# Gated attention and mixture of experts: the residual sum as two fused VectorE operations, the state products as 32-row blocks

## The chip, the cores and the metric

The kernel runs on one core of one Trainium2 chip. The metric is the device time of one execution in microseconds (us); lower is better. The core has the engines TensorE (PE in the profile, with its weight loads as PEld), VectorE (DVE), ScalarE (ACT), GpSimd (POOL) and SyncE (SP), which run side by side and wait for one another by semaphores, and 16 DMA engines.

## What is computed

Inputs are `x` (8 sequences of 512 tokens, 256 wide) and a context of the same shape. The first half, cut to what matters:

```python
q = layernorm(x); k = v = context
ig, fg = gates of [q, k, v], one per head         # 8 heads of 32
cs = cumsum(log_sigmoid(fg)); log_D = causal(cs_s - cs_t + ig_t)
C = (q_h @ k_h.T / sqrt(32)) * exp(log_D - rowmax)
h = (C / (max(|sum C|, exp(-rowmax)) + eps)) @ v_h
x = x + tanh(g0) * layernorm(h) * ln_scale
```

The second half is a mixture of 9 experts (256 to 704 to 256, the two best of 9 per token) on `layernorm(x)`, added with weight `tanh(g1)`.

## The kernel before, in words

**Stages.** A first stage (0 to 57 us) normalises the queries and makes the gate products. A gate stage (57 to about 70 us) makes the cumulative sums and the factors. The **slot loop** (about 77 to 302 us) does the attention for 32 tiles of 128 tokens, tile t = 4b + c being quarter c of sequence b, and beside it splits the experts' weights into two bf16 parts and writes them back to memory. A short routing stage (302 to 350 us) picks experts and builds gather tables. The expert stage (350 to 788 us) gathers tokens, multiplies and scatters, with TensorE nearly always busy.

**The slot loop's order.** The order on each engine is written out by hand in `slot_pe`, `slot_act`, `slot_dve`, `slot_pool` and `slot_sync` (lines 739 to 816). Every engine runs strictly through its own list, slot by slot; there is no planner. A tile is spread over several slots: in slot t, VectorE finishes the attention of tile t (`b_h_dve`), takes statistics of `h` of tile t and of the residual sum of tile t-2 (`c_sth_dve`, `c_stx_dve`), updates the running state of tile t+1 (`b_st_dve`), and multiplies and splits the scores of tile t+2 (`b_c_dve`, `b_cl_dve`: Cm at line 588, Cl at line 596). Line 625, the first operation of `b_h_dve`, is a good mark for where a slot begins on VectorE; it waits for TensorE's products of tile t (lines 522 to 537), which may start only when the `h` of tile t-1 has been taken out of PSUM (`b_ho`).

**ScalarE** in slot t normalises `h` of tile t-1 into `x2` (`c_hn_act`, line 682), normalises tile t-3 into `y`, takes the exponentials of tile t+2, copies, makes the two factors `rs` (`c_rs_act`), casts the scores to bf16 (Ch, line 550) and then casts one 128x1224 piece of the weights (line 468).

**GpSimd** in slot t makes `kw` of tile t+2 (line 569), `qE` of tile t+1 (577), the low part of the values (561), the residual sum of tile t-1 in two operations (`c_pool`: times `lsg` at 717, plus `xc` at 720), and then three operations on the piece of weights that ScalarE just cast (`w_pool`, line 483).

**The state.** For each tile but the last of a sequence, TensorE multiplies `kw` (128 tokens by 4 heads x 32) with the values (128 tokens by 4 heads x 33) for two groups of four heads (lines 498 to 500). Each 128x132 result holds 16 blocks of head by head, of which only the four on the diagonal are wanted. VectorE scales the result and zeroes the rest with the mask `blkm`: for c = 0 straight into the state `St` (line 607), for c = 1 and 2 into `Ut` (line 609), from which two operations update the state (line 615: `St_new = St_old * dec + Ut`). c = 3 has no update. The state is the moving operand of line 522.

**The start.** Constants are made on GpSimd (`consts_pool`) and VectorE (`consts_dve`). ScalarE and TensorE wait for all of them (`s_const` at NCONST) before anything else. In the gate stage, `g_dvef` on VectorE and `g_pool` on GpSimd work at the same time.

The functions that the change touches, and those that call them:

Of the kernel before, what the change touches and what calls it, by code (L numbers as in the profile page):

```python
# [60 lines left out]
def build(nc, x, kv, wgate, fib, lnrow, gsc, wroute, rbias, wts, out):  # L61
    with ExitStack() as ctx:
# [18 lines left out]
        rowj = sb("rowj", [P, P]); rowjb = sb("rowjb", [P, P], BF16); pairj = sb("pairj", [P, HALF]); pcol = sb("pcol", [P, 1]); blk = sb("blk", [P, HG * DV])  # L81
# [4 lines left out]
        selt = sb("selt", [12, HG]); blkm = sb("blkm", [P, HG * DV]); blkt = sb("blkt", [P, HG * DV])  # L86
# [27 lines left out]
        Ut = attn("Ut", [P, 2, HG * DV])  # L114
# [48 lines left out]
        b_kw = sem("b_kw"); b_ut = sem("b_ut"); b_st = sem("b_st")  # L163
# [47 lines left out]
        NCONST = 16  # L211

        def consts_dve(dve):
            nc.vector.memset(eps_c[:, :], LN_EPS).then_inc(s_const, 1)
# [9 lines left out]
            nc.vector.tensor_scalar(blkt[:, :], blk[:, :], float(DH), pcol[:, 0:1], ALU.add, ALU.is_gt).then_inc(s_const, 1)  # L224
            nc.vector.tensor_scalar(blkm[:, :], blk[:, :], pcol[:, 0:1], None, ALU.is_le).then_inc(s_const, 1)
            dve.wait_ge(s_const, 11)
            nc.vector.tensor_tensor(blkm[:, :], blkm[:, :], blkt[:, :], ALU.mult).then_inc(s_const, 1)
# [449 lines left out]
        def c_hn_act(act, t):  # L677
            c = t % NC
            ge(act, c_nb, t + 1)
            ge(act, c_y, t - 3)  # L680
            ge(act, c_x2o[c], 16 * (t // NC))
            nc.scalar.activation(x2[:, c, :], h[:, c, :], ACT.Identity, bias=nb[:, c, 0:1], scale=rs[:, c, 0:1]).then_inc(c_xn, 1)
# [9 lines left out]
        def c_rs_act(act, t):  # L692
# [19 lines left out]

        def c_pool(pool, t):
            G = nc.gpsimd
            b, c = t // NC, t % NC
            ge(pool, c_xn, t + 1)
            G.tensor_tensor(x2[:, c, :], x2[:, c, :], lsg[:, :], ALU.mult).then_inc(c_xa, 1)  # L717
            ge(pool, c_xa, t + 1)
            ge(pool, c_x[b % 2], 16 * (b // 2) + 16)
            G.tensor_tensor(x2[:, c, :], x2[:, c, :], xc[b % 2][:, c, :], ALU.add).then_inc(c_x2, 1)  # L720
# [70 lines left out]
        def slot_pool(pool, t):  # L791
# [646 lines left out]
```

## Time and profile before

| | us |
|---|---|
| median of 3 runs | 788.55 (786.97 to 788.75) |
| the profiled execution, its own time | 790.31 |
| span of the profiled execution | 788.5 |
| VectorE busy | 527.2 (67%) |
| GpSimd busy | 404.8 (51%) |
| TensorE busy | 678.9 (86%) |
| ScalarE busy | 386.1 (49%) |

The profile is of one execution. Busy time is the time in which an engine had an instruction in work; a busy TensorE is not TensorE at its peak, since its instructions overlap. Fp32 products have two records each for the weight load and for the product. The shares above are means over stages with different limits, so a change in the slot loop is read from the slot loop. The granted clock of TensorE is 1.00 for 2.4 GHz and 0.50 for 1.2 GHz.

### The profile page before, as it was taken

What the parts mean: (1) busy time and instruction counts of PE and PEld (TensorE: products, weight loads), DVE (VectorE), ACT (ScalarE), POOL (GpSimd) and SP (SyncE); (2) the same over time, 40 slices, a digit from 0 to 9 for tenths busy, and PEclk for the clock granted to TensorE, in tenths of its full rate; (3) what the DMA queues carried; (4) which work ended last, traced back from release to release, by engine and by line L of the source; (5) the groups of instructions that cost most, each with busy time, mean ns of one, the idle gap of its engine ahead of it and who ended that gap; (6) DMA issues with size and microseconds to landing.
All of it is one profiled execution on the core that took longest, in us unless ns stands there. A gap on an engine that the chain in (4) does not pass through costs nothing.

```text
span 788.5 us, 17816 instructions
## 1 busy us (share of the span) xinstructions
PE 678.9 (86%) x6018; PEld 545.5 (69%) x6018; DVE 527.2 (67%) x1389; ACT 386.1 (49%) x973; POOL 404.8 (51%) x402
## 2 busy tenths in 40 slices
PE   1983889998899874068999999999999999999993
PEld 1541556665566663047998989988989899889893
DVE  8716899899998877964555565555555555655551
ACT  3533677777777763154344444343444443434441
POOL 5024499897989991021244453453444535444423
PEclk9995655557655655569999999999999999999997
DMA  9813789986998861173597897897988977969752
GB/s 283 270 37 122 198 267 263 297 280 208 298 300 254 269 209 54 29 307 108 166 289 238 265 281 253 232 315 213 281 259 245 291 253 234 315 200 305 231 147 49
DMA packets 85817, 179.70 MB, mean 228 GB/s; under 512 B 14881, under 2 KB 48546, under 8 KB 85730
## 3 DMA queue, kind: packets, MB, share of 16 engines
q1 hardware_dynamic: 63202, 140.10, 56.2%
q0 software_dynamic: 13824, 18.43, 10.8%
q10 hardware_dynamic: 8704, 20.06, 6.5%
q8 instruction: 48, 0.79, 0.4%
q14 instruction: 39, 0.32, 0.1%
HBM read 140.93 MB, written 38.67 MB: 228 GB/s over the span
## 4 chain that ended last, share of the span: by engine, by line
PE 57%; POOL 20%; issue 9%; DVE 9%; ACT 2%; DMA 2%; SPq 1%; POOLq 0%; DVEq 0%; ACTq 0%
PE bank L1096 49%; POOL whl L483 8%; POOL x L717 3%; POOL x L720 3%; POOL vp L561 3%; POOL qE L577 2%; PE bank L304 2%; PE bank L1090 2%; PE bank L307 2%; POOL kw L569 2%; DVE R L991 1%; PE bank L317 1%; DMA EB<-e_d 1%; DVE Qe L988 1%; PE bank L734 1%
## 5 line engine op out<-in xcount | busy, mean ns | idle before, releaser
L1096 PE MATMUL bank<-xh,w 128*128 128x256 bf16 (+1 forms) x1760 | 268.2, 263 | 9.7 <-DVE xl L1152 5.7
L1078 POOL DMA_INDIRECT out<-res,TS x72 | 115.4, 1603 | 214.9 <-DVE res L1213 130.9
L1096 PE MATMUL bank<-xl,w 128*128 128x256 bf16 (+1 forms) x880 | 222.5, 263 | 0.0
L1169 ACT ACTIVATE sg<-bank 128x256 f32<-128x256 f32 (+1 forms) x240 | 86.8, 362 | 230.3 <-PE bank L1096 226.6
L1096 PEld LDWEIGHTS bank<-xh,w 128*128 128x128 bf16 x1760 | 165.5, 98 | 28.5 <-issue 11.9
L1199 DVE TENSOR_TENSOR hf<-sg,bank 128x256 f32<-128x256 f32 (+1 forms) x200 | 78.9, 394 | 122.5 <-ACT sg L1169 117.4
L1096 PE MATMUL bank<-w,hh 128*128 128x256 bf16 x864 | 140.0, 273 | 0.0
L483 POOL TENSOR_TENSOR whl<-wst,whl 128x408 bf16<-128x408 f32 x96 | 94.0, 1006 | 61.2 <-ACT whl L468 61.1
L1069 POOL DMA_INDIRECT xg<-y_d,TG x72 | 72.7, 1010 | 79.0 <-DVE TS L1026 48.4
L1096 PE MATMUL bank<-w,hlo 128*128 128x256 bf16 x360 | 98.1, 273 | 0.0
L1163 ACT CAST hh<-hf 128x256 bf16<-128x256 f32 (+1 forms) x240 | 90.4, 377 | 12.9 <-DVE hf L1201 11.6
L1096 PEld LDWEIGHTS bank<-xl,w 128*128 128x128 bf16 x880 | 86.4, 98 | 8.3
L1096 PEld LDWEIGHTS bank<-w,hh 128*128 128x128 bf16 x864 | 84.5, 98 | 9.3
L1185 DVE TENSOR_TENSOR hlo<-hf,hh 128x256 bf16<-128x256 f32 (+1 forms) x200 | 78.3, 392 | 0.0
L596 DVE TENSOR_TENSOR Cl<-Cm,Ch 128x512 bf16<-128x512 f32 x64 | 60.3, 979 | 7.3 <-ACT Ch L550 5.0
L1213 DVE TENSOR_SCALAR res<-bank,cws 128x256 f32<-128x256 f32 x72 | 31.8, 479 | 43.2 <-PE bank L1096 43.2
L550 ACT CAST Ch<-Cm 128x512 bf16<-128x512 f32 x64 | 37.0, 617 | 39.6 <-DVE Cm L588 39.6
L510 PE MATMUL bank<-maskb,identb 128*128 128x512 bf16 x64 | 36.3, 567 | 14.4 <-ACT Dm L544 10.0
L588 DVE SCALAR_TENSOR_TENSOR Cm<-bank,Dm 128x512 f32<-128x512 f32 x64 | 41.1, 680 | 7.6 <-ACT Dm L544 7.6
L734 PEld LDWEIGHTS bank<-wr,yT 128*128 128x128 f32 x128 | 27.8, 303 | 20.8 <-ACT yT L706 11.4
L468 ACT CAST whl<-wst 128x1224 bf16<-128x1224 f32 x32 | 38.6, 1209 | 4.2 <-DMA w_d<-whl 4.2
L734 PE MATMUL bank<-wr,yT 128*128 128x9 f32 x128 | 30.7, 351 | 9.0 <-ACT yT L706 8.0
(222 smaller groups left out, 1107.4 us busy)
## 6 DMA issues: line engine op xcount, KB each, us to landing
w<-w_d SPq DMA_DIRECT2D x40, 1408.0 KB
w<-w_d SPq DMA_DIRECT2D x40, 768.0 KB
wst<-in_wts SPq DMA_DIRECT2D x32, 612.0 KB, 4.7
w_d<-whl ACTq DMA_DIRECT2D x32, 612.0 KB, 6.7
vb<-in_kv SPq DMA_DIRECT2D x8, 528.0 KB, 5.4
xa<-in_x SPq DMA_DIRECT2D x8, 512.0 KB, 8.5
kT<-in_kv SPq DMA_DIRECT2D x8, 512.0 KB, 8.9
xc<-in_x SPq DMA_DIRECT2D x8, 512.0 KB, 7.7
```

Of the source, the lines that this page charges most:

```text
L468: nc.scalar.copy(whl[w][:, 0, :], wst[w][:, :]).then_inc(w_hi, 1)
L483: ins = nc.gpsimd.tensor_tensor(whl[w][:, 1, cols], wst[w][:, cols], whl[w][:, 0, cols], ALU.subtract)
L588: nc.vector.scalar_tensor_tensor(by4(Cm[t % 2][g][:, :]), bank[:, 4:8, g * P:(g + 1) * P], SCALE, by4(Dm[t % 2][g][:, :]), ALU.mult, ALU.m ...
L596: nc.vector.tensor_tensor(Cl[k][:, :], Cm[t % 2][g][:, :], Ch[k][:, :], ALU.subtract).then_inc(b_Cl, 1)
L734: mm = nc.tensor.matmul(bank[:, 3, LG0 + c * NE:LG0 + (c + 1) * NE], yT[t % 2][:, k, :], wr[:, k, :], start=(k == 0), stop=(k == KD - 1))
L1069: nc.gpsimd.indirect_dma_start(xg[w][:, j, :], None, y_d, bass.IndirectOffsetOnAxis(ap=TG[:, c0:c0 + 1], axis=0)).then_inc(f_xg[w], 16)
L1078: nc.gpsimd.indirect_dma_start(out, bass.IndirectOffsetOnAxis(ap=TS[:, c0:c0 + 1], axis=0), res[w][:, j, :], None, bounds_check=TOK - 1, o ...
L1096: mm = nc.tensor.matmul(dst, l, r, start=(n == 0), stop=(n == len(pairs) - 1))
L1163: nc.scalar.copy(hh[w][0:K, m, 0:N], hf[m % 3][0:K, 0:N]).then_inc(f_hh, 1)
L1169: nc.scalar.activation(sg[m % 2][0:K, 0:N], bank[0:K, 2 + (NM * w + m) % 4, 0:N], ACT.Silu).then_inc(f_sg, 1)
L1185: V.tensor_tensor(hl_[w][:, m, 0:N], hf[m % 3][:, 0:N], hh[w][:, m, 0:N], ALU.subtract).then_inc(f_hl, 1)
L1199: V.tensor_tensor(hf[m % 3][:, 0:N], sg[m % 2][:, 0:N], bank[:, bk, SLOT:SLOT + N], ALU.mult).then_inc(f_hf, 1)
```

## The change

Two things change in the slot loop.

1. `c_hn_act` on ScalarE and `c_pool` on GpSimd go. In their place, `c_x2_dve` on VectorE makes `x2 = (h - mean) * lsg` and `x2 = x2 * rs + xc`, two `scalar_tensor_tensor` operations of 128x256, the second waiting for the first. It stands in `slot_dve` right behind `b_h_dve`, for tile t-1.
2. The state product is made by eight products of 32 output rows and 33 columns, one per head, straight into the diagonal blocks. The rest of the PSUM region is zeroed once, in the gate stage. The mask, `Ut` and line 609 go, the update reads PSUM directly, and the factor SCALE moves into the copy that makes `col` (line 348). With the mask go one `iota` on GpSimd and three operations on VectorE among the constants, and NCONST is 13.

```diff
+            V.memset(bank[:, 4:6, UO:UO + HG * DV], 0.0).then_inc(b_uz, 1)
...
-                    nc.scalar.copy(dst, src).then_inc(g_cols, 1)
+                    nc.scalar.activation(dst, src, ACT.Copy, scale=SCALE).then_inc(g_cols, 1)
...
                 for g in range(2):
-                    mm = nc.tensor.matmul(bank[:, 4 + g, UO:UO + HG * DV], kw[u % 2][:, g * P:(g + 1) * P],
-                                          vv(u)[:, g * HG * DV:(g + 1) * HG * DV], start=True, stop=True)
+                    for j in range(HG):
+                        hd = g * HG + j
+                        mm = nc.tensor.matmul(bank[DH * j:DH * (j + 1), 4 + g, UO + DV * j:UO + DV * (j + 1)],
+                                              kw[u % 2][:, DH * hd:DH * (hd + 1)], vv(u)[:, DV * hd:DV * (hd + 1)],
+                                              start=True, stop=True)
...
                 ub = bank[:, 4:6, UO:UO + HG * DV]
-                mask = blkm[:, :].unsqueeze(1).to_broadcast([P, 2, HG * DV])
+                ge(dve, b_h, t)
                 if c == 0:
-                    ge(dve, b_h, t)
-                    V.scalar_tensor_tensor(St[0][:, :, :], ub, SCALE, mask, ALU.mult, ALU.mult).then_inc(b_st, 1)
+                    V.tensor_copy(St[0][:, :, :], ub).then_inc(b_st, 1)
                 else:
-                    V.scalar_tensor_tensor(Ut[:, :, :], ub, SCALE, mask, ALU.mult, ALU.mult).then_inc(b_ut, 1)
                     if t == 1:
                         ge(dve, s_dec, 16 * HG)
-                    ge(dve, b_ut, b * 2 + c)
-                    ge(dve, b_h, t)
                     for g in range(2):
                         ins = V.scalar_tensor_tensor(St[c % 2][:, g, :], St[1 - c % 2][:, g, :], dec[:, b, g, c:c + 1],
-                                                     Ut[:, g, :], ALU.mult, ALU.add)
+                                                     ub[:, g, :], ALU.mult, ALU.add)
...
+        def c_x2_dve(dve, t):
+            V = nc.vector
+            b, c = t // NC, t % NC
+            ge(dve, c_rs, t + 1)
+            ge(dve, c_mv2, t + 1)
+            ge(dve, c_y, t - 3)
+            ge(dve, c_x2o[c], 16 * b)
+            V.scalar_tensor_tensor(x2[:, c, :], h[:, c, :], mv[:, c, 0, 0:1], lsg[:, :], ALU.subtract, ALU.mult).then_inc(c_xn, 1)
+            ge(dve, c_xn, t + 1)
+            ge(dve, c_x[b % 2], 16 * (b // 2) + 16)
+            V.scalar_tensor_tensor(x2[:, c, :], x2[:, c, :], rs[:, c, 0:1], xc[b % 2][:, c, :], ALU.mult, ALU.add).then_inc(c_x2, 1)
...
         def slot_dve(dve, t):
             if 0 <= t < NT:
                 b_h_dve(dve, t)
+            if 0 <= t - 1 < NT:
+                c_x2_dve(dve, t - 1)
             if 0 <= t < NT:
                 c_sth_dve(dve, t)
```

The calls of `c_hn_act` in `slot_act` and of `c_pool` in `slot_pool` are removed with the functions.

## Rows read from the trace of the kernel before

**Rows 1.** Busy us (x count) of PE, PEld, DVE, ACT, POOL; PEclk, DMA, GB/s

```profile
95.80:291.20 195.40, 179.89 (x1571) 122.52 (x1567) 177.41 (x422) 148.47 (x314) 176.55 (x210) 0.56 0.87 268
110.00:153.00 43.00, 41.92 (x340) 28.09 (x336) 39.33 (x95) 32.33 (x68) 38.88 (x47) 0.50 0.96 295
...
258.00:265.00 7.00, 4.62 (x57) 2.92 (x56) 6.79 (x17) 5.18 (x11) 5.28 (x8) 0.97 1.03 317
```

**Rows 2.** Chain of waits of the slot loop, shares by line

```profile
by line: POOL whl L483 29.0%; issue 25.2%; POOL x L717 11.3%; POOL x L720 10.5%; POOL vp L561 9.5%; POOL qE L577 8.0%; POOL kw L569 6.5%; POOLq L182 0.4%
```

**Rows 3.** Line 607, one in four slots: min/median/max, first and last start

```profile
L607 DVE SCALAR_TENSOR_TENSOR St<-bank,blkm x8: 415/433/433, 81.4 to 270.7; 128x264 f32<-128x264 f32 x8
```

**Rows 4.** VectorE in order of time: start, us, line; from 199.71 one whole slot

```profile
199.71 0.15 DVE L625 SCALAR_TENSOR_TENSOR n<-bank,col 128x8 f32<-128x8 f32 x1
...
200.34 0.42 DVE L632 TENSOR_TENSOR h<-bank,n 128x256 f32<-128x256 f32 x1
...
201.88 0.40 DVE L609 SCALAR_TENSOR_TENSOR Ut<-bank,blkm 128x264 f32<-128x264 f32 x1
202.31 1.09 DVE L615 SCALAR_TENSOR_TENSOR St<-St,dec,Ut 128x132 f32<-128x132 f32 x2
203.33 1.27 DVE L588 SCALAR_TENSOR_TENSOR Cm<-bank,Dm 128x512 f32<-128x512 f32 x2
...
204.82 1.79 DVE L596 TENSOR_TENSOR Cl<-Cm,Ch 128x512 bf16<-128x512 f32 x2
206.53 0.15 DVE L625 SCALAR_TENSOR_TENSOR n<-bank,col 128x8 f32<-128x8 f32 x1
...
217.57 2.20 DVE L596 TENSOR_TENSOR Cl<-Cm,Ch 128x512 bf16<-128x512 f32 x2 [0.15 <-ACT Ch L550]
```

**Rows 5.** VectorE again, where GpSimd was idle

```profile
87.14 0.62 DVE L615 SCALAR_TENSOR_TENSOR St<-St,dec,Ut 128x132 f32<-128x132 f32 x2
...
288.17 1.29 DVE L596 TENSOR_TENSOR Cl<-Cm,Ch 128x512 bf16<-128x512 f32 x2
```

**Rows 6.** GpSimd in order of time

```profile
204.73 0.73 POOL L720 TENSOR_TENSOR x<-x,xc 128x256 f32<-128x256 f32 x1
206.45 2.81 POOL L483 TENSOR_TENSOR whl<-wst,whl 128x408 bf16<-128x408 f32 x3 [0.99 <-ACT whl L468]
```

**Rows 7.** ScalarE in order of time

```profile
288.51 1.21 ACT L468 CAST whl<-wst 128x1224 bf16<-128x1224 f32 x1
```

**Rows 8.** VectorE by line and shape, whole span: busy us, mean ns

```profile
L1185 DVE TENSOR_TENSOR hlo<-hf,hh 128x256 bf16<-128x256 f32 x160 | 66.8, 418 | 0.0
L596 DVE TENSOR_TENSOR Cl<-Cm,Ch 128x512 bf16<-128x512 f32 x64 | 60.3, 979 | 7.3 <-ACT Ch L550 5.0
...
L1213 DVE TENSOR_SCALAR res<-bank,cws 128x256 f32<-128x256 f32 x72 | 31.8, 479 | 43.2 <-PE bank L1096 43.2
...
L615 DVE SCALAR_TENSOR_TENSOR St<-St,dec,Ut 128x132 f32<-128x132 f32 x32 | 18.6, 622 | 0.6
```

**Rows 9.** TensorE in order of time at the half clock

```profile
210.12 1.02 PE L734 MATMUL bank<-wr,yT 128*128 128x9 f32 x4
...
213.15 1.24 PE L493 MATMUL bank<-qT,kT 32*128 32x128 f32 x16
214.32 1.25 PE L499 MATMUL bank<-vb,kw 128*128 128x132 f32 x4
```

**Rows 10.** GpSimd, then VectorE, in the constants at the start

```profile
6.93 3.65 POOL L208 MEMSET mx<- 24x4096 bf16 x1
...
7.05 3.61 DVE L225 TENSOR_SCALAR blkm<-blk,pcol 128x132 f32<-128x132 f32 x1
10.70 0.30 DVE L227 TENSOR_TENSOR blkm<-blkm,blkt 128x132 f32<-128x132 f32 x1
```

**Rows 11.** VectorE in the gate stage

```profile
63.79 0.17 DVE L384 MEMSET g<- 64x128 f32 x1
63.89 1.36 DVE L385 TENSOR_TENSOR g<-gm 64x384 f32<-64x384 f32 x1
```

More of the change, by code:

```diff
@@ L78, in build @@
         bank = ctx.enter_context(nc.psum_tensor("bank", [P, 8, 512], F32))
-        rowj = sb("rowj", [P, P]); rowjb = sb("rowjb", [P, P], BF16); pairj = sb("pairj", [P, HALF]); pcol = sb("pcol", [P, 1]); blk = sb("blk", [P, HG * DV])
+        rowj = sb("rowj", [P, P]); rowjb = sb("rowjb", [P, P], BF16); pairj = sb("pairj", [P, HALF]); pcol = sb("pcol", [P, 1]);
         tokp1 = sb("tokp1", [P, NT])
@@ L85, in build @@
         maskb = sb("maskb", [P, P], BF16); sel12 = sb("sel12", [12, HG])
-        selt = sb("selt", [12, HG]); blkm = sb("blkm", [P, HG * DV]); blkt = sb("blkt", [P, HG * DV])
+        selt = sb("selt", [12, HG]);
         eps_c = sb("eps_c", [P, 1]); neps_c = sb("neps_c", [P, 1]); revj = sb("revj", [P, NE]); one_c = sb("one_c", [P, 1])
@@ L113, in build @@
         kw = [attn(f"kw{w}", [P, D]) for w in range(2)]; St = [attn(f"St{w}", [P, 2, HG * DV]) for w in range(2)]
-        Ut = attn("Ut", [P, 2, HG * DV])
         n1 = attn("n1", [P, NH]); n2 = attn("n2", [P, NH]); n3 = attn("n3", [P, NH])
@@ L162, in build @@
         b_dl = sem("b_dl"); b_s = sem("b_s"); b_D = sem("b_D"); b_C = sem("b_C")
-        b_kw = sem("b_kw"); b_ut = sem("b_ut"); b_st = sem("b_st")
+        b_kw = sem("b_kw"); b_uz = sem("b_uz"); b_st = sem("b_st")
         b_h = sem("b_h"); b_n = sem("b_n"); b_ho = sem("b_ho")
@@ L168, in build @@
         c_x = [sem(f"c_x{w}") for w in range(2)]; c_st2 = sem("c_st2"); c_mv2 = sem("c_mv2"); c_st3 = sem("c_st3"); c_mv3 = sem("c_mv3")
-        c_nb = sem("c_nb"); c_lv = sem("c_lv"); c_rs = sem("c_rs"); c_xa = sem("c_xa"); c_xn = sem("c_xn"); c_x2 = sem("c_x2"); c_y = sem("c_y"); c_yT = sem("c_yT"); c_yc = sem("c_yc")
+        c_nb = sem("c_nb"); c_lv = sem("c_lv"); c_rs = sem("c_rs"); c_xn = sem("c_xn"); c_x2 = sem("c_x2"); c_y = sem("c_y"); c_yT = sem("c_yT"); c_yc = sem("c_yc")
         c_lp = sem("c_lp"); c_lg = sem("c_lg"); c_x2o = [sem(f"c_x2o{c}") for c in range(NC)]; c_yo = [sem(f"c_yo{c}") for c in range(NC)]
@@ L199, in consts_pool @@
                            allow_small_or_imprecise_dtypes=True).then_inc(s_iota, 1)
-            nc.gpsimd.iota(blk[:, :].rearrange("p (h e) -> p h e", e=DV), [[DH, HG], [0, DV]], base=0,
-                           channel_multiplier=0, allow_small_or_imprecise_dtypes=True).then_inc(s_iota, 1)
             nc.gpsimd.iota(tokp1[:, :], [[P, NT]], base=1, channel_multiplier=1,
@@ L209, in consts_pool @@
                 nc.gpsimd.memset(asb[w][:, :, :], 1.0).then_inc(s_mz, 1)
-        NCONST = 16
+        NCONST = 13
         def consts_dve(dve):
@@ L217, in consts_dve @@
             nc.vector.memset(onesb[:, :], 1.0).then_inc(s_const, 1)
-            dve.wait_ge(s_iota, 5)
+            dve.wait_ge(s_iota, 4)
             nc.vector.tensor_copy(rowjb[:, :], rowj[:, :]).then_inc(s_const, 1)
@@ L223, in consts_dve @@
             nc.vector.tensor_scalar(maskb[:, :], rowj[:, :], pcol[:, 0:1], NEG, ALU.is_lt, ALU.mult).then_inc(s_const, 1)
[L224 to L227, printed above, removed]
+            dve.wait_ge(s_const, 9)
             nc.vector.tensor_tensor(selt[:, :], identf[0:12, 0:4], identf[0:12, 4:8], ALU.add).then_inc(s_const, 1)
-            dve.wait_ge(s_const, 13)
+            dve.wait_ge(s_const, 10)
             nc.vector.tensor_tensor(sel12[:, :], selt[:, :], identf[0:12, 8:12], ALU.add).then_inc(s_const, 1)
@@ L358, in g_pe_all @@
             mm.then_inc(g_col, 1)
+            pe.wait_ge(b_uz, 1)
             b_s_pe(pe, 0)
@@ L675, in c_nb_dve @@
             nc.vector.scalar_tensor_tensor(nb[:, r, lo:hi], mv[:, r, lo:hi, 0], -1.0, rs[:, r, lo:hi], ALU.mult, ALU.mult).then_inc(c_nb, 1)
[L677 to L682, printed above, removed]
+        def c_x2_dve(dve, t):
[9 more added lines that the diff above has]
+            V.scalar_tensor_tensor(x2[:, c, :], x2[:, c, :], rs[:, c, 0:1], xc[b % 2][:, c, :], ALU.mult, ALU.add).then_inc(c_x2, 1)
         def c_y_act(act, t):
@@ L696, in c_rs_act @@
             ge(act, c_mv3, t - 1)
-            ge(act, c_xn, t - 3)
+            ge(act, c_x2, t - 3)
             ge(act, c_y, t - 5)
@@ L711, in c_lg_act @@
                            bank[:, 3, LG0:LG0 + NC * NE]).then_inc(c_lg, 1)
[L713 to L720, printed above, removed]
         def c_T_pe(pe, t):
@@ L751, in slot_act @@
         def slot_act(act, t):
-            if 0 <= t - 1 < NT:
-                c_hn_act(act, t - 1)
             if 0 <= t - 3 < NT:
@@ L797, in slot_pool @@
                 b_v_pool(pool, t + 1)
-            if 0 <= t - 1 < NT:
-                c_pool(pool, t - 1)
             if t in PIECE:
```

## The prediction

> **What bounds the kernel now.** The change touches the slot loop and a little of the start, so I first asked for the busy time of that loop alone. Over 195.4 us VectorE is busy 177.4, GpSimd 176.6 and TensorE 179.9 [rows 1]: three engines at about 91%, ScalarE at 76%. No single engine is clearly the bound, and the page's shares for the whole span (67% and 51%) hide this. TensorE runs the loop mostly at a granted clock of about half (mean 0.56); where it was 0.50 throughout, TensorE was busy 41.92 of 43.00 us, where it was 0.97 only 4.62 of 7.00 [rows 1]. The chain of waits lies on GpSimd from end to end, 29.0% on line 483 and 21.8% on the two operations that the change removes [rows 2]. That invites the reading "unload GpSimd and the loop gets faster". Whether it holds depends on what the other engines have left, so I took the pitch of the loop: line 607 runs once in four slots, eight times from 81.4 to 270.7, which is 189.3 / 28 = 6.76 us a slot [rows 3].
>
> Next, VectorE in order of time [rows 4]. In the slot from 199.71 to 206.53 it has no idle time of note: 2.17 us from line 625 to line 609, 1.45 for Ut and the two state operations, 1.49 from Cm to Cl, 1.71 for the two Cl. So VectorE has no room for more work; only the length of its own operations can give.
>
> They can give, for this reason: an operation of VectorE with two SBUF operands waits while GpSimd's is in work. The pair of Cl took 1.29 us and the pair of St 0.62 where GpSimd was idle [rows 5], but 1.79 and 1.09 in the slot above [rows 4]. The Cl pair of 204.82 shows how: GpSimd's line 720 ran from 204.73 to 205.46 and then GpSimd was idle until 206.45 [rows 6], and the pair was longer by just the rest of that one operation. Over all slots Cl has a mean of 979 ns against some 0.65 alone, St 622 against 0.31 [rows 5, 8]. In the constants the same shows at its largest: line 225 stood 3.61 us behind GpSimd's memset of 3.65 [rows 10].
>
> **The change, part by part**, per slot on VectorE.
>
> 1. Two new operations. A 128x256 operation with two SBUF operands alone took 418 ns (line 1185); a pointer scalar adds about 60, by line 1213 (479) [rows 8]. So 2 x 0.48, and 0.05 for the hand-over between them: +1.0.
> 2. What they wait for GpSimd. The pair starts 1.05 us behind line 625 (200.34 + 0.42 against 199.71) [rows 4]. When does GpSimd's burst of line 483 start? It follows ScalarE's weight cast, which ended at 289.72 where the Cl pair ended at 289.46 [rows 5, 7], so about 0.3 us behind the start of the slot, now that nothing else keeps GpSimd. The burst is 2.8 us long [rows 6]. So the pair falls into it in every slot: the first operation waits for the rest of one 0.94 us operation (some 0.2 to 0.4), and the second, which may start only when the first is done, for most of the next (0.5). Bounds: 0 if they miss the burst, and 1.2 (the Cl pair of 217.57 took 2.20, 0.9 more than alone [rows 4, 5], beside operations of 0.73; beside those of 0.94 that is 0.9 x 0.94 / 0.73). I take +0.8, as the phase puts the pair inside.
> 3. Ut goes: 0.43 in half of the slots [rows 4]: -0.2.
> 4. St reads PSUM instead of Ut and no longer has two SBUF operands. As the Cm of line 588, which also mixes PSUM and SBUF and keeps 1.27 for its pair [rows 4], it should keep its length alone. From 2 x 0.62 to 0.62 in half of the slots [rows 5, 8]: -0.3. For c = 0 a copy replaces an operation of 433 ns [rows 3]: 0.
> 5. Cl. GpSimd's list shrinks by two operations of 0.73 alone [rows 6], from about 6.1 us (176.6 in the 28.9 slots of [rows 1]) to 4.5, plus some 0.8 that it waits for the pair. It starts at 0.3 and ends near 5.6, while the Cl pair starts 1.3 us before the end of the slot. So Cl is free: from 2 x 0.98 to 1.29: -0.65 [rows 5, 8].
> 6. Idle time of VectorE that the longer list absorbs: -0.1.
>
> Sum: 1.0 + 0.8 - 0.2 - 0.3 - 0.65 - 0.1 = +0.55, say +0.5 a slot, over some 30 slots **+15 us**. The other moves: `c_hn_act` leaves ScalarE, which had 24% idle, so 0; its place in the list is ahead of work that waits for VectorE anyway. No DMA is added or moved; the store of `x2` waits for the same sum, which now comes at most a slot later or earlier, with two slots to spare. New waits (`c_rs`, `c_mv2`, the stores) are for things of the slot before: 0. What queues behind the pair is the statistics, then `rs` on ScalarE, then Cm; `rs` is wanted only behind Cm: 0.
>
> **TensorE.** At the half clock it is busy 41.92 of 43.00 us [rows 1], 6.6 a slot, so it is as full as VectorE. Eight products of a quarter width replace two. The nearest row is line 493: eight products on a quarter of the array each, 16 records in 1.24 us [rows 9], about what line 499 takes now. I take 0. Below: 0.3, a quarter of line 499's 1.25, if four run side by side; that gain would be hidden behind VectorE. Above: 4.1, if each costs like a product of line 734, of which two, with few columns, take 1.02 [rows 9]. With a slot of 7.3 TensorE has 0.7 left, over three products in four slots 0.9 for each: it stays hidden up to some 2.1 us.
>
> **The start.** VectorE's line 227 (0.30) goes, with an iota of GpSimd ahead of its memsets. Line 225 goes too, but line 229 behind it has two SBUF operands and would stand behind the same memset [rows 10]: -0.3 for line 227; the iota comes on top, unpriced. The new memset in the gate stage (264 columns; the one ahead of it, of 128, took 0.17, so about 0.3) goes ahead of line 385, which took 1.36 us, mostly a wait for GpSimd [rows 11]; that wait covers it: 0, and +0.3 without this cover.
>
> **Sum.** 15 - 0.3 = +14.7. The profiled execution took 790.31 (span 788.5), 1.8 above the median; from it 805.0, and against the median of 788.55, 803.
>
> **A rule weighed.** Alone, an operation of two SBUF operands took 0.645 us with 512 columns (the Cl pair halved) and 0.418 with 256, 0.89 ns a column, which gives 0.31 for 132; the St pair, of the new operations' form, took 0.31 each [rows 5, 8]. At half the rate it would be 0.42. The Trainium skill, Vector Engine (DVE) Microarchitecture Reference, "Points that are easy to get wrong", says that this form of instruction with two SBUF sources that aren't bf16 runs at half the throughput. By it each new operation would be longer by 256 columns' time, and the sum about 14 us higher; by the rows it is not. This is the third rival below.
>
> **The rivals.**
> - *The pair misses the burst* (faster). Place: 1.05 us into a VectorE slot. If the weight cast comes late on ScalarE, or the slot's start is early, the pair runs while GpSimd is idle, at 1.0. Then the slot is 6.76 + 1.0 - 0.2 - 0.3 - 0.65 = 6.6, or -5 us in all with the start: 783. It decides at 0.3 us of wait for the pair. For it: GpSimd's share of busy time falls to about 70%. Against: the phase of rows 5 and 7. Chance 0.17.
> - *Nothing to measure*: the wait for the pair is 0.2 to 0.4: 786 to 791. Chance 0.13.
> - *Half throughput* in the new operations: 256 columns more at 0.89 ns, 0.23 each, 0.46 a slot, +14 on top: 817. Against: the St pair. Chance 0.06.
> - *TensorE becomes the bound*: the eight products take more than 2.1 us at the half clock. Halfway to the upper bound, at 2.6, a slot takes 6.6 + 0.75 x (2.6 - 1.2) = 7.65: +0.9 over 30 slots, 815; at 4.1 it is 8.8 a slot, 850. Against: rows 9, line 493. Chance 0.05.
> - My forecast: 0.59.
>
> That the change does nothing is no rival: the operations leave GpSimd by name.
>
> **The numbers.** Forecast 803. The range of 785 to 815 holds my forecast with its bounds (a pair's wait of 0.4 to 1.2), the case of no difference and the edge of the first rival; it leaves out the rest of that and most of the last two, 0.2. A measurement here can tell 0.3% from no change, 2.4 us. Faster 0.17, no difference 0.13, slower 0.59 + 0.06 + 0.05 = 0.70.
>
> **What would show it.** GpSimd's busy time in the loop down by some 50 us. Line 596 at a mean near 0.7 us, line 615 near 0.33. The two new operations at 0.48 alone but 0.7 to 1.0 in the mean, more in the second. The pitch of four slots near 29 us, with VectorE waiting for nobody. Wrong would be: the pair at 1.0 to 1.2 (first rival), VectorE idle before line 625 behind TensorE (the last), or Cl still near 1.0, which would add up to 0.65 a slot.

## The result, and the profile after

The changed kernel takes **791.82 us** (median of 20 runs, 788.08 to 801.65), the kernel before 788.46 in runs beside it (20 runs, 785.82 to 790.64). The 801.65 is a slow execution, at a granted clock of 0.794 where the other 19 have 0.814 to 0.834, and the ratio leaves it out. The ratio is 1.0041, with a 95% interval of 1.0028 to 1.0055: slower by 0.41%, just more than the 0.3% that a measurement here can tell. The forecast was 803 with a range of 785 to 815. The direction and the range held; the size did not: +3.4 us where the sum said +14.7.

The profiled execution of the changed kernel took 794.40 us (span 792.3), 2.6 above the median; that of the kernel before lies 1.8 above its own, so the two traces can be compared.

The busy time of the slot loop, in the columns of [rows 1], over the same stretch:

```profile
95.80:291.20 195.40, 164.41 (x1792) 107.58 (x1788) 183.56 (x458) 133.45 (x284) 129.93 (x152) 0.59 0.86 267
```

GpSimd went from 176.6 us to 129.9, -46.7 where some -50 was forecast, and VectorE from 177.4 to 183.6 of 195.4. TensorE fell from 179.9 to 164.4. VectorE is now the one full engine. The chain of waits from 95.8 to 245 says so too; in [rows 2] nearly every share was GpSimd's, and in the list below none is. (Over the whole stretch of [rows 2], 95.8 to 292, the chain has 8.7% on GpSimd's line 479 and 13.2% on Cl.)

```profile
by line: issue 25.0%; DVE Cl L595 17.3%; DVE x L679 9.6%; ACT Ch L549 8.0%; DVE st L648 5.6%; DVE Cm L587 5.1%; ACTq L470 3.4%; DVE st L657 3.3%; DVE n L624 3.0%; DVE n L622 2.5%; DVEq L181 2.1%; DVE x L682 1.9%; ACT lv L699 1.8%; DVE mv L6
```

(The list goes on behind its last entry.) The pitch by the line that runs once in four slots [rows 3] is (273.4 - 80.8) / 28 = 6.88 us against 6.76:

```profile
L605 DVE COPY St<-bank x8: 411/413/433, 80.8 to 273.4; 128x264 f32<-128x264 f32 x8
```

One slot of VectorE in order of time, to be read against [rows 4], and beside it GpSimd, to be read against [rows 6]:

```profile
200.05 0.42 DVE L627 TENSOR_TENSOR h<-bank,n 128x256 f32<-128x256 f32 x1
200.39 0.69 DVE L679 SCALAR_TENSOR_TENSOR x<-h,mv,lsg 128x256 f32<-128x256 f32 x1
201.11 1.06 DVE L682 SCALAR_TENSOR_TENSOR x<-x,rs,xc 128x256 f32<-128x256 f32 x1
202.10 0.41 DVE L648 BATCH_NORM_STATS2 st<-h 128x6 f32<-128x256 f32 x1
...
203.17 0.59 DVE L610 SCALAR_TENSOR_TENSOR St<-St,dec,bank 128x132 f32<-128x132 f32 x2
203.68 1.28 DVE L587 SCALAR_TENSOR_TENSOR Cm<-bank,Dm 128x512 f32<-128x512 f32 x2
...
205.18 1.29 DVE L595 TENSOR_TENSOR Cl<-Cm,Ch 128x512 bf16<-128x512 f32 x2
206.39 0.16 DVE L620 SCALAR_TENSOR_TENSOR n<-bank,col 128x8 f32<-128x8 f32 x1
```

```profile
199.84 3.15 POOL L479 TENSOR_TENSOR whl<-wst,whl 128x408 bf16<-128x408 f32 x3 [1.91 <-ACT whl L464]
202.95 0.72 POOL L576 TENSOR_TENSOR qE<-qT,EB 128x256 f32<-128x256 f32 x1
203.64 0.68 POOL L560 TENSOR_TENSOR vp<-vb,vp 128x264 bf16<-128x264 f32 x1
```

The slot starts at 199.42 (the first n of line 620), the burst at 199.84, 0.42 us in (forecast: 0.3). The pair of new operations (lines 679 and 682) lies wholly inside it. It takes 202.10 - 200.39 = 1.71 us from its start to the start of what follows. Where GpSimd was idle, at the end of the loop, the same pair took 0.91:

```profile
297.40 0.42 DVE L627 TENSOR_TENSOR h<-bank,n 128x256 f32<-128x256 f32 x1
297.75 0.47 DVE L679 SCALAR_TENSOR_TENSOR x<-h,mv,lsg 128x256 f32<-128x256 f32 x1
298.26 0.48 DVE L682 SCALAR_TENSOR_TENSOR x<-x,rs,xc 128x256 f32<-128x256 f32 x1
298.66 0.42 DVE L648 BATCH_NORM_STATS2 st<-h 128x6 f32<-128x256 f32 x1
```

GpSimd pays for the meeting too: three operations of line 479 take 3.15 us here against 2.81 in [rows 6]. The Cl pair, by contrast, runs after GpSimd's list has ended (204.32) and takes its 1.29. The means over all slots agree (VectorE, 96 to 292; columns as in [rows 8], where the means are of the whole span). First the kernel before, then the changed one:

```profile
L596 DVE TENSOR_TENSOR Cl<-Cm,Ch 128x512 bf16<-128x512 f32 x58 | 56.0, 1005 | 7.0 <-ACT Ch L550 5.0
...
L615 DVE SCALAR_TENSOR_TENSOR St<-St,dec,Ut 128x132 f32<-128x132 f32 x28 | 16.7, 635 | 0.5
...
L625 DVE SCALAR_TENSOR_TENSOR n<-bank,col 128x8 f32<-128x8 f32 x29 | 4.7, 160 | 3.8 <-PE bank L536 3.2
```

```profile
L595 DVE TENSOR_TENSOR Cl<-Cm,Ch 128x512 bf16<-128x512 f32 x56 | 36.6, 695 | 5.3 <-ACT Ch L549 2.9 <-PE bank L535 0.2
...
L682 DVE SCALAR_TENSOR_TENSOR x<-x,rs,xc 128x256 f32<-128x256 f32 x28 | 29.1, 1041 | 1.0
L679 DVE SCALAR_TENSOR_TENSOR x<-h,mv,lsg 128x256 f32<-128x256 f32 x29 | 19.6, 676 | 0.0
...
L610 DVE SCALAR_TENSOR_TENSOR St<-St,dec,bank 128x132 f32<-128x132 f32 x28 | 8.3, 339 | 0.0
...
L620 DVE SCALAR_TENSOR_TENSOR n<-bank,col 128x8 f32<-128x8 f32 x28 | 4.5, 160 | 0.3 <-PE bank L535 0.3
```

The last column is idle time of VectorE before the operation: its wait for TensorE at the start of a slot fell from 3.8 us to 0.3, and its wait ahead of Cl from 7.0 to 5.3.

**Where the time went.** A record's duration is not the time that it holds up the engine, because records overlap (run 6 below has 0.39 us of record in 0.31 of time). So the account is in times from start to start, as means over all slots from 96 to 292 in the timeline of VectorE:

| us a slot | before | after | difference |
|---|---|---|---|
| first n to h | 0.63 | 0.63 | 0 |
| h to the statistics of h (with the pair) | 0.46 | 2.02 | +1.56 |
| the statistics | 1.18 | 1.11 | -0.07 |
| state update (with Ut, before) to Cm | 0.87 | 0.35 | -0.52 |
| Cm to Cl | 1.70 | 1.61 | -0.08 |
| Cl to the next n | 2.02 | 1.24 | -0.78 |
| pitch | 6.86 | 6.96 | +0.10 |

The ends of the loop do the rest. The first n comes 0.37 us earlier (84.25 against 84.62); the last state copy, at 273.4, 2.7 later; the last n (296.77 against 295.35) only 1.4 later, as the last slots take less time than before; and what follows the loop on VectorE (302.93 against 300.61) 2.3 later. The first gather of the expert stage keeps these 2.3 (351.38 against 349.07). The spans differ by 3.8 (792.3 and 788.5), so 1.5 arises in the expert stage, which the change doesn't touch and which no run took apart; the spans of 19 executions of the changed kernel lie up to 6 us apart (786.2 to 792.3), so these 1.5 may be no effect of the change.

TensorE's side of the change, in order of time, against [rows 9]:

```profile
213.20 1.24 PE L489 MATMUL bank<-qT,kT 32*128 32x128 f32 x16
214.37 0.45 PE L497 MATMUL bank<-vb,kw 128*32 128x33 f32 x16
214.75 0.61 PE L509 MATMUL bank<-maskb,identb 128*128 128x512 bf16 x1
```

The eight products take 214.75 - 214.37 = 0.38 us, start to start; two of full width took 1.04 (the next operation began at 215.36 after 214.32), both at a granted clock of 0.50.

### The profile page after: what moved, and what is told of

The parts are those of the page before. It is cut to its first block, busy times and chain, and to the rows that moved or that the text cites. A ratio compares the mean times of both kernels' runs of the same rounds, so it can differ in the third digit from the quotient of the medians.

```text
span 792.3 us, 18373 instructions
## 1 busy us (share of the span) xinstructions
PE 665.5 (84%) x6306; PEld 531.9 (67%) x6306; DVE 538.3 (68%) x1435; ACT 371.6 (47%) x941; POOL 353.9 (45%) x337
## 4 chain that ended last, share of the span: by engine, by line
PE 54%; DVE 21%; issue 10%; ACT 4%; DMA 4%; POOL 4%; ACTq 1%; DVEq 0%; SPq 0%; POOLq 0%
PE bank L1085 44%; DVE Cl L595 4%; DMA out<-res,TS 4%; POOL whl L479 2%; DVE x L679 2%; PE bank L298 2%; PE bank L301 2%; ACT Ch L549 2%; PE bank L1079 1%; DVE Cm L587 1%; DVE st L648 1%; DVE R L980 1%; PE bank L311 1%; DVE xl L1141 1%; PE bank L725 1%
## 5 line engine op out<-in xcount | busy, mean ns | idle before, releaser
L479 POOL TENSOR_TENSOR whl<-wst,whl 128x408 bf16<-128x408 f32 x96 | 99.5, 1064 | 110.8 <-ACT whl L464 107.3
L595 DVE TENSOR_TENSOR Cl<-Cm,Ch 128x512 bf16<-128x512 f32 x64 | 42.4, 702 | 5.8 <-ACT Ch L549 2.9
L489 PE MATMUL bank<-qT,kT 32*128 32x128 f32 x512 | 39.2, 450 | 1.2 <-DVE Cm L587 1.2
```

The lines of the kernel that those rows point to most:

```text
L479: ins = nc.gpsimd.tensor_tensor(whl[w][:, 1, cols], wst[w][:, cols], whl[w][:, 0, cols], ALU.subtract)
L489: mm = nc.tensor.matmul(bank[:, 4 + j, g * P:(g + 1) * P], kT[rows, b, c, g * P:(g + 1) * P], qT[rows, b, c, g * P:(g + 1) * P], start=Tru ...
L595: nc.vector.tensor_tensor(Cl[k][:, :], Cm[t % 2][g][:, :], Ch[k][:, :], ALU.subtract).then_inc(b_Cl, 1)
```

## The experiments

The kernel before ran beside every group of runs, at a median of 788.7 to 788.9. The diffs are cut to the lines that matter; where a run leaves out or adds more than its diff shows, the text says so. The means from start to start come from VectorE's timeline as in the table above.

**1. The residual sum alone.** The kernel before, with only the residual sum moved to VectorE (`c_hn_act` goes as well); the state product with mask and Ut stays.

```
         def slot_dve(dve, t):
             if 0 <= t < NT:
                 b_h_dve(dve, t)
+            if 0 <= t - 1 < NT:
+                c_x2_dve(dve, t - 1)
...
-            if 0 <= t - 1 < NT:
-                c_pool(pool, t - 1)
```

> The kernel before with the residual sum on VectorE alone; state product, mask and Ut as before. Theory A (VectorE's list sets the pitch of the slot loop, and the new pair costs it 0.80 us alone plus 0.76 of waiting for GpSimd's burst): the pitch is that of the changed kernel, 6.96 us, plus Ut (0.43 in half of the slots) and the St pair's wait (0 to 0.3), so 7.2 to 7.4, and the time 797 to 804 us. Theory B (another engine, TensorE above all, holds the pitch near 6.9, and VectorE only fills it): 789 to 793, the same as the changed kernel.

Measured: 809.18 us, 1.0261 [1.0235 to 1.0288]; pitch 7.47. That is above the range of the theory, and far from its rival. The theory gave Ut 0.2 us a slot and the St pair's wait 0 to 0.3. VectorE's timeline has more:

```profile
202.96 0.67 DVE L684 SCALAR_TENSOR_TENSOR x<-h,mv,lsg 128x256 f32<-128x256 f32 x1
203.66 1.06 DVE L687 SCALAR_TENSOR_TENSOR x<-x,rs,xc 128x256 f32<-128x256 f32 x1
...
205.72 0.40 DVE L609 SCALAR_TENSOR_TENSOR Ut<-bank,blkm 128x264 f32<-128x264 f32 x1
206.16 1.49 DVE L615 SCALAR_TENSOR_TENSOR St<-St,dec,Ut 128x132 f32<-128x132 f32 x2
```

The state update, which reads two SBUF operands here, stands in its turn behind GpSimd: 1.49 us for what took 0.62 alone [rows 5]. From the first state operation to Cm it is 0.90 us a slot in the mean, against 0.35 in the changed kernel. From Cl to the next n it is 1.22, and VectorE waits for TensorE nowhere at the start of a slot (0.0 us), though TensorE still makes the two full products. The residual sum by itself costs 20.5 us, not 3.4. The changed kernel is nearly level only because its other half pays for it.

**2. The state blocks alone.** The changed kernel, with the residual sum put back to ScalarE and GpSimd.

```
-            V.scalar_tensor_tensor(x2[:, c, :], h[:, c, :], mv[:, c, 0, 0:1], lsg[:, :], ALU.subtract, ALU.mult).then_inc(c_xn, 1)
...
+            nc.scalar.activation(x2[:, c, :], h[:, c, :], ACT.Identity, bias=nb[:, c, 0:1], scale=rs[:, c, 0:1]).then_inc(c_xn, 1)
...
+            G.tensor_tensor(x2[:, c, :], x2[:, c, :], lsg[:, :], ALU.mult).then_inc(c_xa, 1)
```

> The kernel before with the state product in 32-row blocks alone; the residual sum stays on ScalarE and GpSimd. Theory A: VectorE is relieved of Ut (0.2 a slot) and of the St pair's wait (0.3), so the pitch goes from 6.86 to 6.4 to 6.6, time 777 to 783 us; GpSimd, busy 6.1 us a slot, is the next limit and may keep part of it. Theory B: TensorE is relieved too, by 0.66 us in three of four slots (eight products took 0.38 where two took 1.04), so 0.5 a slot, and the time also falls, but then TensorE shows idle time of less than 0.3 us a slot.

Measured: 778.69 us, 0.988 [0.9851 to 0.9909], as the theory said; again, later (label e12), 779.58, 0.9891 [0.9864 to 0.9917]:

> The same kernel as e2_state_only: 778 to 780 us, 1.2% under the kernel before.

The loop in the columns of [rows 1], then VectorE's Cl by line:

```profile
95.80:281.00 185.20, 168.63 (x1790) 111.93 (x1790) 167.72 (x405) 146.65 (x312) 181.30 (x210) 0.55 0.90 280
```

```profile
L595 DVE TENSOR_TENSOR Cl<-Cm,Ch 128x512 bf16<-128x512 f32 x56 | 60.8, 1124 | 10.8 <-ACT Ch L549 9.0
```

The pitch is 6.56 and GpSimd is busy 181.3 of 185.2 us (168.1 before): now it is the fullest engine. VectorE saved 0.51 between update and Cm, and 0.28 came back: 0.17 from Cm to Cl, where the wait for ScalarE's Ch has grown from 5.0 to 9.0 us, and 0.11 from Cl to n. Cl has a mean of 1124 ns, against 1013 in the kernel before over the same stretch (96 to 281); GpSimd was in work during 1.08 us of a Cl operation in the mean, during 0.77 before. The run relieves TensorE too, by 0.66 us in three slots of four, and how much of the 10 us is due to that, it doesn't show. So the two halves of the change don't add: -10 and +20.5 alone (+10.5), +3.4 together.

**3. The pair at another place.** The changed kernel, with the pair moved from behind h to ahead of Cl.

```
         def slot_dve(dve, t):
             if 0 <= t < NT:
                 b_h_dve(dve, t)
-            if 0 <= t - 1 < NT:
-                c_x2_dve(dve, t - 1)
...
                 c_nb_dve(dve, t)
+            if 0 <= t - 1 < NT:
+                c_x2_dve(dve, t - 1)
             if 0 <= t + 2 < NT:
```

> The changed kernel with the two operations of the residual sum moved from behind b_h_dve to ahead of the Cl pair in VectorE's list, where GpSimd was idle in the trace. Theory A: the pair takes 0.48 + 0.48 us instead of 0.68 + 1.04, Cl stays near 0.65 to 0.75 each, the pitch falls by 0.5 to 0.75 to 6.2 to 6.45, time 773 to 780 us. Theory B: the pair is as short, but VectorE shows the time as idle (ahead of line 620, behind TensorE), and the time stays at 786 to 792.

Measured: 781.49 us, 0.9912 [0.9887 to 0.9938], 10 us less than the changed kernel, with the same instructions; 1.5 above the range expected. VectorE's timeline shows a slot where the pair meets the end of GpSimd's list, and the next, where it doesn't; the second fence is GpSimd:

```profile
200.36 0.55 DVE L670 SCALAR_TENSOR_TENSOR nb<-mv,rs 128x2 f32<-128x2 f32 x1
200.84 0.98 DVE L679 SCALAR_TENSOR_TENSOR x<-h,mv,lsg 128x256 f32<-128x256 f32 x1
201.86 0.48 DVE L682 SCALAR_TENSOR_TENSOR x<-x,rs,xc 128x256 f32<-128x256 f32 x1
...
208.14 0.15 DVE L670 SCALAR_TENSOR_TENSOR nb<-mv,rs 128x2 f32<-128x2 f32 x1
208.21 0.48 DVE L679 SCALAR_TENSOR_TENSOR x<-h,mv,lsg 128x256 f32<-128x256 f32 x1
208.72 0.48 DVE L682 SCALAR_TENSOR_TENSOR x<-x,rs,xc 128x256 f32<-128x256 f32 x1
```

```profile
200.16 0.73 POOL L576 TENSOR_TENSOR qE<-qT,EB 128x256 f32<-128x256 f32 x1
200.85 0.69 POOL L560 TENSOR_TENSOR vp<-vb,vp 128x264 bf16<-128x264 f32 x1
...
206.57 0.68 POOL L560 TENSOR_TENSOR vp<-vb,vp 128x264 bf16<-128x264 f32 x1
```

At 208.21 GpSimd has been idle since 207.25 and both operations take 0.48. At 200.84 the first stands beside vp of line 560 and is 0.50 us longer. It is the same pair, and only GpSimd's work beside it differs. In this kernel VectorE is busy 177.4 of 185.2 us and its idle time, but for the hand-overs of some 0.03 us between its own operations, is 1.0 us in all: VectorE's list, with what is left of its waits for GpSimd inside it, sets this pitch of 6.52. The Trainium skill, SBUF — State Buffer, "Who interferes with whom", says that a VectorE instruction with two SBUF inputs contends with a GpSimd instruction that reads SBUF, and that the issue order decides which of the two waits. The meetings shown here agree; and the update with a PSUM operand kept its length: 343 ns in run 3, with GpSimd in work beside it, 338 in run 4, with GpSimd nearly always idle beside it.

**4. A short burst.** The changed kernel; from the third weight piece on GpSimd works out 8 of each 408 columns of the weights' low parts, and the rest of the low parts is left out.

```
-                cols = slice(i * third, (i + 1) * third)
+                cols = slice(i * third, i * third + (8 if n > 1 else third))
```

> The changed kernel, order untouched, but from the third piece of weights on GpSimd's three operations of a piece work on 8 columns each instead of 408, so that most of the low parts are left out. Theory A: the pair takes 0.48 + 0.48 us where it stands, the pitch falls by 0.7 to 6.2 to 6.3, time 769 to 776 us. Theory B: at least 786.

Measured: 781.98 us, 0.9914 [0.9889 to 0.994]: a miss of 6 us. Short as the burst is, what follows it on GpSimd now meets the pair. VectorE, then GpSimd:

```profile
208.73 0.79 DVE L679 SCALAR_TENSOR_TENSOR x<-h,mv,lsg 128x256 f32<-128x256 f32 x1
209.56 0.48 DVE L682 SCALAR_TENSOR_TENSOR x<-x,rs,xc 128x256 f32<-128x256 f32 x1
```

```profile
208.15 0.51 POOL L479 TENSOR_TENSOR whl<-wst,whl 128x8 bf16<-128x8 f32 x3 [3.98 <-ACT whl L464]
208.63 0.61 POOL L568 TENSOR_TENSOR kw<-vb,col 128x256 f32<-128x256 f32 x1
```

The time from h to the statistics fell from 2.02 only to 1.76 us. GpSimd was busy 62.9 of 185 us instead of 124, and two thirds of the pair's wait were still there (824 and 645 ns in the mean where 0.48 us each is the length alone, 0.51 us a slot against 0.76): what stands beside the pair counts, not how full GpSimd is.

**5, 6 and 10. How much does a longer list of VectorE cost?** One more statistics operation of 0.39 us (bn_stats into a tile that nobody reads), behind the two of the slot: in the kernel before (run 5), in the changed kernel (run 6), and in the changed kernel with a wait for it (run 10).

```
                 c_stx_dve(dve, t - 2)
+                nc.vector.bn_stats(st9[:, t % NC, :], h[:, (t - 2) % NC, :])
```

Run 10 adds the wait:

```
-                nc.vector.bn_stats(st9[:, t % NC, :], h[:, (t - 2) % NC, :])
+                nc.vector.bn_stats(st9[:, t % NC, :], h[:, (t - 2) % NC, :]).then_inc(c_ex, 1)
+                ge(dve, c_ex, t - 1)
```

> The kernel before with one more bn_stats of 128x256 per slot on VectorE (32 of them, into a tile that nobody reads), behind c_stx_dve; it has one SBUF operand and takes 0.40 us. It prices VectorE's time in the kernel before. Theory A (the three engines share the limit before: part of a longer VectorE list is taken out of its idle time and of the Cl pair's wait): +0.15 to 0.3 a slot, 793 to 798 us. Rival (VectorE alone sets the pitch): the full 0.4, 801 us. Rival (VectorE is hidden): 789.

> The changed kernel with the same extra bn_stats. Theory A (in the changed kernel VectorE alone sets the pitch, since its waits for other engines are gone): the full 0.38 to 0.4 a slot, +12 us over the changed kernel, 803 to 805 us. Rival (TensorE at the half clock shares it): +4 to 8, 796 to 800.

> As e6_after_extra, but VectorE's next operation waits for the extra bn_stats by a semaphore. In e6 the extra operation of 394 ns moved the next group by only 0.28 us, and the time by 3.9. Theory C (a record's length is not the room it takes: an operation that nobody waits for overlaps its neighbours by about 0.1 us, one that is waited for does not): here it takes 0.42 to 0.46 a slot and the time is 3 to 5 us above e6's, 799 to 801. Rival (the 0.28 is all it takes, the rest was absorbed elsewhere): 796, as e6.

"In its phase" is what the stretch from the statistics to the state update gained, "given back" what the named stretch lost, in us a slot:

| run | us | ratio to before | in its phase | given back elsewhere | pitch |
|---|---|---|---|---|---|
| 5, before | 791.63 | 1.0047 [1.0025, 1.0069] | +0.22 | 0.17 (Cl to n) | +0.06 |
| 6, changed | 795.73 | 1.0093 [1.0076, 1.011] | +0.28 | 0.09 (Cm to Cl) | +0.16 |
| 10, changed, waited for | 799.56 | 1.0147 [1.0121, 1.0173] | +0.40 | 0.12 (Cm to Cl) | +0.27 |

Runs 5 and 6 cost about 4 us each (0.0047 x 788 = 3.7, and 795.73 - 791.82 = 3.9) where 30 times 0.39 would be 12. Run 5 missed its range (793 to 798) by 1.4. There are two reasons, and both apply to the sum of the prediction. First, the record of an operation that nothing waits for overlaps the next. Run 6, then run 10, in VectorE's timeline:

```profile
203.98 0.39 DVE L773 BATCH_NORM_STATS2 st<-h 128x6 f32<-128x256 f32 x1
204.29 0.60 DVE L610 SCALAR_TENSOR_TENSOR St<-St,dec,bank 128x132 f32<-128x132 f32 x2
```

```profile
206.34 0.39 DVE L773 BATCH_NORM_STATS2 st<-h 128x6 f32<-128x256 f32 x1
206.77 0.61 DVE L610 SCALAR_TENSOR_TENSOR St<-St,dec,bank 128x132 f32<-128x132 f32 x2
```

The same 0.39 takes 0.31 here without a wait and 0.43 with one. Second, VectorE's own waits shrink by part of what is added. In run 5 about half of the 0.17 lies inside Cl (its mean falls from 1013 to 976 ns), the rest is the wait for TensorE at the start of a slot (3.8 us in all before, 1.4 now). But the profiled execution of run 5 is a quick one (789.97, 1.7 under its median), with TensorE at a granted clock of 0.64 in the loop against 0.56, so its +0.06 is less than the median time tells (3.7 us in 31 slots, 0.12 a slot), and how much of the shorter wait is the clock's, the run doesn't show. Run 6 missed its range of 803 to 805, and its rival (796 to 800) by a little; run 10 was forecast from these two findings, and its time came out as forecast (799 to 801), its 0.40 a slot a little under the forecast 0.42 to 0.46.

**7 and 9. Part of the work moved.** The kernel of run 2 (kernel 2), with the residual sum of one tile in four (run 7) or of every second tile (run 9) on VectorE ahead of Cl, as two operations with ScalarE's part kept.

```
+            if 0 <= t - 1 < NT and (t - 1) % NC == 1:
+                c_x2_dve(dve, t - 1)
...
-            if 0 <= t - 1 < NT:
+            if 0 <= t - 1 < NT and (t - 1) % NC != 1:
                 c_pool(pool, t - 1)
```

Run 9 has `% 2 == 1` and `% 2 == 0` in their place.

> The state product in 32-row blocks, and the residual sum left on ScalarE and GpSimd, but for one tile in four (c = 1), whose two GpSimd operations go to VectorE ahead of the Cl pair, in the slot that has no state update. Theory A (in e2_state_only GpSimd, busy 6.28 of 6.55 us a slot, sets the pitch together with VectorE): GpSimd gets 0.37 less a slot, VectorE 0.2 more; pitch 6.3 to 6.45, 772 to 776 us. Rival (TensorE at the half clock holds it): 778 to 780, as e2_state_only.

> As e7_mixed with two tiles in four (c = 1 and 3) summed on VectorE. Theory A: GpSimd gets 0.37 less a slot than in e7, VectorE 0.2 more; between e7 (6.49) and e3_x2_late (6.52) in kind, so with both engines off their limit 6.35 to 6.45: 772 to 776 us. Rival (TensorE at the half clock, busy 169.2 of 185 us in e7, holds the pitch): 776 to 779.

Measured: 776.22 us for run 7, 0.9867 [0.9819 to 0.9914], 0.2 above its range; again (label e11) 776.4, 0.9855 [0.983 to 0.988]; 777.14 for run 9, 0.9852 [0.9827 to 0.9876], 1.1 above its range and inside its rival's.

> The same kernel as e7_mixed, on the same chip as e12_state_again, to rank the two. Theory A: 775 to 777, 2 us under e12. Rival: no difference.

The loop of run 7 and of run 9, in the columns of [rows 1]:

```profile
95.80:281.00 185.20, 169.44 (x1819) 114.19 (x1818) 170.84 (x419) 147.88 (x314) 171.01 (x198) 0.55 0.90 281
```

```profile
95.80:281.00 185.20, 162.25 (x1820) 109.82 (x1820) 172.64 (x436) 147.64 (x314) 154.82 (x185) 0.60 0.89 283
```

GpSimd loses 10 us of busy time from kernel 2 to run 7, and the pitch falls from 6.56 to 6.49 (6.44 in the second execution of the same kernel, label e11); another 16 us, in run 9, bring 6.45 and no shorter time. **Runs 7 and 9 are the fastest kernels found**, and the runs can't tell them apart: 1.4% under the one before, 2% under the changed one. Kernel 2 is 2.5 us above run 7 the first time and 3.2 the second, with intervals that overlap.

**8. The weights' low parts a slot later.** The kernel of run 3, with GpSimd's burst one slot behind ScalarE's cast, so that it need not wait for it, and, not in the diff, ScalarE's Ch ahead of the store.

```
-            if t in PIECE:
-                w_pool(pool, PIECE[t])
+            if t - 1 in PIECE:
+                w_pool(pool, PIECE[t - 1])
```

> As e3_x2_late (the pair ahead of Cl), and GpSimd's burst on a piece of weights comes a slot later in its list, so that it no longer waits for ScalarE's cast of the same slot; ScalarE issues the write behind Ch instead of ahead of it. Theory A (what is left of waiting in e3 is GpSimd's operations meeting the pair and Cl): GpSimd's list of some 4.6 us then runs from the start of the slot and is done before the pair, which falls from 0.72 + 0.49 to 0.48 + 0.48, and Cl from 0.79 to 0.65; pitch 6.0 to 6.25, 768 to 773 us. Rival (TensorE at the half clock, about 6.1 to 6.3 of work a slot, holds it): 776 to 781, with VectorE idle ahead of line 620.

Measured: 800.25 us, 1.0154 [1.0137 to 1.0171]: a miss of 27 us. The list of waits of GpSimd, and two lines of VectorE:

```profile
POOL vp L560 <- ACT vp L555: 72.4, 26, 6.8
```

```profile
L679 DVE SCALAR_TENSOR_TENSOR x<-h,mv,lsg 128x256 f32<-128x256 f32 x26 | 28.1, 1081 | 0.0
...
L670 DVE SCALAR_TENSOR_TENSOR nb<-mv,rs 128x2 f32<-128x2 f32 x26 | 13.3, 513 | 0.0
```

The burst lost one wait, and vp ahead of it took another: 72.4 us for ScalarE's copy, with the burst queued behind it. It ends on the pair, whose first operation now takes 1081 ns. The copy is late because ScalarE is held too: its cast of the next piece waits 14.5 us for the burst and 7.6 us for the store behind it (1.8 us for the store in run 3, nothing for the burst), and the copy stands behind the cast. So the two engines wait for each other in a ring. That follows from their lists and waits; no run broke the ring.

## Why the prediction came out as it did

- **What bounds the kernel**: right in the main. Unloading GpSimd gave nothing by itself; in the changed kernel GpSimd waits 61.8 us for ScalarE's cast and nobody gains by it. But "no room for more work" was too strong. An added 0.39 us raised the pitch of the kernel before by 0.06 in the trace and some 0.12 by the median (run 5); its waits ahead of n and inside Cl were room.
- **Term 2**, the pair's wait for GpSimd (+0.8): right. 1.56 - 0.80 = 0.76, in the operations and in the order named: the first about 0.2, the second the rest. One reading behind it was loose: the Cl pair of 204.82 was not longer "by just the rest" of GpSimd's operation, which was 205.46 - 204.82 = 0.64, but by 0.50. In run 3 it is the same: 201.54 - 200.84 = 0.70 of vp were left, and the operation was 0.50 longer.
- **Terms 3 and 4**, Ut and the state update (-0.5): right, -0.52. Run 2 has -0.51 for them without the pair.
- **Term 1 failed**: "2 x 0.48, and 0.05 for the hand-over between them: +1.0". The 0.48 was right, partly by luck, since line 1213, from which the 60 ns for the pointer scalar came, differs from line 1185 also in reading PSUM. But the pair alone costs 0.80. The records run 0.08 into what follows (298.66 - 298.26 = 0.40 for 0.48), and the hand-over from h to its statistics goes: 0.46 from h to the statistics before, 0.35 from h to the pair now, because the pair reads the h of the slot before and so waits for nothing, while the statistics of h no longer follow it directly. Durations were taken as the time that an operation occupies its engine.
- **Term 5**, Cl (-0.65): right. From 2 x 1005 to 2 x 695 ns over the same slots is -0.62.
- **Term 6 failed**: "idle time of VectorE that the longer list absorbs: -0.1". Terms 5 and 6 together measured -0.93 (-0.78 from Cl to n, -0.08 from Cm to Cl, -0.07 in the statistics), which leaves -0.31 for term 6. The idle times above hold 0.19 of it (3.8 + 7.0 - 0.3 - 5.3 = 5.2 us in 28 slots), the wait ahead of Ut and line 607, now gone, is part of the 0.07 in the statistics. The prediction had no row for its 0.1. Could the shorter products of TensorE have done this, and not the longer list? Not alone: in run 1, which has the long list and the old products, VectorE's wait for TensorE is gone as well (0.0 us) and Cl to n is 1.22.
- **The sum**: 1.8 - 0.5 - 0.75 = +0.55 forecast, 1.56 - 0.52 - 0.93 = +0.11 measured. Each term was off by 0.21 or less, and the result by over three quarters, since it is a small difference of large terms. Over 30 slots the two failed terms are 30 x (0.20 + 0.21) = 12.3 us, somewhat more than the 11.3 that the prediction was off; the sum had also rounded 0.55 down to 0.5.
- **TensorE at 0**: right. The eight products save 0.66 us in three slots of four, more than the lower bound of 0.3 below which nothing was thought likely, and the gain is hidden behind VectorE, as the prediction said of any gain there: VectorE waits 0.3 us in all for TensorE at the start of its slots, and 0.0 in run 1 without the gain.
- **The start**: right, -0.37 at the first slot against -0.3. The memset of the gate stage is covered: the operation behind it ends at 65.31 where it ended at 65.25.
- **The rivals.** That the pair misses the burst: its wait is 0.76, above the 0.3 from which it decides, so no; but run 3 shows the rival's mechanism with the pair elsewhere, at 781. Half throughput: 0.48 alone for 256 columns, so no. The Trainium skill's rule for this form (Vector Engine (DVE) Microarchitecture Reference, "Points that are easy to get wrong") is not borne out by any row here. TensorE as the bound: no. "Nothing to measure" (786 to 791) was nearest in size and wrong in mechanism: the pair waits its full wait, and other terms pay for it.

**What stays open.** What holds the pitch at 6.44 to 6.49 in runs 7 and 9. In run 3 it is VectorE, which has no idle time left. In kernel 2 GpSimd is fullest (181.3 of 185.2). In run 7 VectorE is busy 170.8, GpSimd 171.0 and TensorE 169.4 of 185.2. TensorE at the half clock is a rival that isn't settled: in the second trace of the same kernel (label e11) it is busy 164.4 at a granted clock of 0.59, and in run 9 162.3 at 0.60, against 0.55, and the pitch is 6.44 and 6.45 against 6.49. No run took work from TensorE alone. Open too are the 1.5 us of the expert stage.

## What to carry to other kernels

When two engines keep each other waiting, ask of a moved operation not only how long it is but what the other engine does at its new place: here the same two operations cost 20 us beside the old state blocks, and beside the new ones (779 us without them) 13 at one place of the slot and 2 at another. Count an operation from start to start, in a place where it is free, not by its record; and where the answer is a small difference of large terms, try a neighbour of the change (one half alone, one operation doubled) before trusting the sum. Idle time of the fullest engine, and what its operations spend waiting inside their own duration, is room: a longer list takes up part of it first, so price that term too, and not by a guess.

## What the runs showed of the hardware

- An operation of VectorE with a record of 0.39 us moves the next by 0.31 if nothing waits for it, by 0.43 if the next does (runs 6 and 10).
- The size of an operation doesn't save it from GpSimd: nb, 128 by 2 with two SBUF operands, takes 0.15 us alone and had a mean of 513 ns in run 8, up to 978.
- An operation with one of its two operands in PSUM isn't held by GpSimd: the state update took 343 ns beside it (run 3) and 338 without it (run 4).
- Relief of one operation can come back in the next: the Cl operations rose from 1013 to 1124 ns when VectorE's list grew shorter (run 2).
- Eight fp32 products of 128 by 32 by 33, each into its own 32 rows, took 0.38 us at a granted clock of 0.50, where two of 128 by 128 by 132 took 1.04.
